# One call instead of two for each head pair's output product in an attention kernel

## The reference, cut to what matters

```python
scores = jnp.einsum('bhqd,bhkd->bhqk', Q, K) / np.sqrt(dh)
x = scores.transpose(0, 2, 1, 3).reshape(b * s, h, s)
x = lax.conv_general_dilated(x, conv_w, window_strides=(1,), padding=[(1, 1)],
                             dimension_numbers=('NCW', 'OIW', 'NCW')) + conv_b[None, :, None]
weights = jax.nn.softmax(x.reshape(b, s, h, s).transpose(0, 2, 1, 3), axis=-1)
out = jnp.einsum('bhqk,bhkd->bqhd', weights, V).reshape(b, s, e) @ Wo.T + bo
```

## Time and profile before

| | us |
|---|---|
| device time, median of 3 runs | 270.06 (269.82 to 270.51) |
| profiled execution, first to last instruction (span) | 268.3 |
| what lies around the span | about 1.8 |
| PE busy in the span | 258.0 (96%) |
| DVE busy | 214.0 (80%) |
| ACT busy | 165.2 (62%) |
| POOL busy | 142.3 (53%) |

### The profile page before, as it was taken

The page is one execution under the profiler, slowest core; times in us unless marked ns, Lnnn a source line. Parts: engine busy times, 40 slices in busy tenths (PEclk is TensorE's granted clock), DMA queues, the critical chain, the costliest instruction groups (busy, mean ns, idle before and its releaser), DMA issues.

```text
span 268.3 us, 5678 instructions
## 1 busy us (share of the span) xinstructions
PE 258.0 (96%) x1835; PEld 191.3 (71%) x1835; DVE 214.0 (80%) x524; ACT 165.2 (62%) x292; POOL 142.3 (53%) x166
## 2 busy tenths in 40 slices
PE   8996989999999999999999999999999999999994
PEld 7455766777777677777667667777676766779982
DVE  2559997988889798888968999889888975686553
ACT  2743887768676776866683577777767771314321
POOL 1029988678687867768482667687863100000000
PEclk9999999999999999999999999999999999999999
DMA  7992000000000000000000000000000000000002
GB/s 222 370 418 85 2 1 1 4 0 0 0 0 0 0 0 0 2 1 2 0 0 2 0 2 0 2 2 0 0 0 0 2 0 2 0 0 4 0 2 78
DMA packets 2964, 8.11 MB, mean 30 GB/s; under 512 B 258, under 2 KB 1794, under 8 KB 2690
## 3 DMA queue, kind: packets, MB, share of 16 engines
q1 hardware_dynamic: 2514, 7.22, 7.2%
q10 hardware_dynamic: 432, 0.65, 0.7%
HBM read 7.34 MB, written 0.52 MB: 29 GB/s over the span
## 4 chain that ended last, share of the span: by engine, by line
PE 82%; DVE 10%; POOL 4%; issue 2%; ACT 1%; DVEq 0%; POOLq 0%; ACTq 0%
PE tp L902 18%; PE sc L777 12%; PE pvbank L794 10%; PE sc L778 9%; PE sc L779 9%; DVE Pb L515 3%; PE sc L993 3%; PE tp L1003 3%; PE sc L721 2%; PE misc L815 2%; DVE PT L631 1%; PE sc L739 1%; PE sc L953 1%; DVE kc L459 1%; PE sc L954 1%
## 5 line engine op out<-in xcount | busy, mean ns | idle before, releaser
L319 ACT ACTIVATE Pb<-Pb,nbias 128x512 f32<-128x512 f32 x128 | 90.7, 721 | 51.5 <-DVE Pb L515 51.0
L515 DVE TENSOR_SCALAR_CACHE_REDUCE Pb<-sc,col 128x512 f32<-128x512 f32 x128 | 93.6, 744 | 19.0 <-PE sc L779 18.3
L902 PE MATMUL tp<-cst,Pb 128*128 128x128 f32 x512 | 76.9, 273 | 0.9 <-DVE PT L631 0.8
L902 PEld LDWEIGHTS tp<-cst,Pb 128*128 128x128 f32 x512 | 63.0, 140 | 20.4 <-issue 1.7
L777 PE MATMUL sc<-Kh,Ql 128*128 128x512 f32 x124 | 60.7, 490 | 0.9 <-POOL Kl L216 0.9
L216 POOL TENSOR_TENSOR Kl<-kc,Kh 128x512 fp32r<-128x512 f32 x29 | 37.5, 1294 | 37.9 <-ACT Kh L314 37.7
L778 PE MATMUL sc<-Kl,Qh 128*128 128x512 f32 x124 | 49.2, 397 | 0.0
L779 PE MATMUL sc<-Kh,Qh 128*128 128x512 f32 x124 | 49.0, 396 | 0.0
L631 DVE COPY PT<-tp 128x512 f32<-128x512 f32 x64 | 43.9, 685 | 1.0 <-PE tp L902 1.0
L228 POOL TENSOR_TENSOR td<-ta,tc_ 128x512 f32<-128x512 f32 x31 | 42.0, 1356 | 2.6
L361 ACT ACTIVATE PT<-tp 128x512 f32<-128x512 f32 x64 | 37.4, 585 | 3.2 <-PE tp L902 2.4
(11 more groups left out here) (232 smaller groups left out, 259.7 us busy)
## 6 DMA issues: line engine op xcount, KB each, us to landing
w1s<-in_w SPq DMA_DIRECT2D x1, 2048.0 KB, 9.6
w2s<-in_w SPq DMA_DIRECT2D x1, 2048.0 KB, 14.0
cst<-in_consts SPq DMA_DIRECT2D x1, 648.0 KB, 5.1
xTs<-in_xT SPq DMA_DIRECT2D x2, 256.0 KB, 3.0
we<-in_wexp SPq DMA_DIRECT2D x2, 256.0 KB, 3.4
b2s<-in_b2row SPq DMA_DIRECT2D x1, 512.0 KB, 14.8
out<-PT SPq DMA_DIRECT2D x2, 192.0 KB, 2.1
wq<-in_wqkvo ACTq DMA_DIRECT2D x1, 320.0 KB, 3.7
```

The costliest lines, as they stand in the source:

```text
L319: act.activation(Pb[:, k, :], Pb[:, k, :], ACT.Exp, bias=nbias[:, k:k + 1], scale=-1.0)\
L515: dve.tensor_scalar(Pb[:, k, :], SC[k % 4][:, :], cb, None, ALU.subtract, ALU.min, accum_out=nbias[:, k:k + 1]).then_inc(s["mx"], 1)
L902: mm = pe.transpose(TP[u % 2][:, k * 128:(k + 1) * 128], Pb[:, u % RING, k * 128:(k + 1) * 128], ident)
```

## The change

A pair's product is one call of `outputs` in u = 1 and in u = 9. It goes through all four tiles of keys, 16 matmul calls or eight rounds, and counts the semaphore `pv` at its end. The calls in u = 3 and 11 are gone. The call's waits are those of the former first half. All other code is the same.

```diff
-            def outputs(hd, j, gi, tiles):
+            def outputs(hd, j, gi):
...
-                for k in tiles:
+                for k in range(QT):
...
-                if k == QT - 1:
-                    mm.then_inc(s["pv"], 1)
+                mm.then_inc(s["pv"], 1)
...
-                if u % (2 * QT) in (1, 3) and not (isinstance(g, int) and b + g == 0 and u < QT):
-                    outputs(H * b + G * g + u // QT - 2, (u // QT - 2) % G, gi - (1 if u < QT else 0),
-                            (0, 1) if u % QT == 1 else (2, 3))
+                if u % (2 * QT) == 1 and not (isinstance(g, int) and b + g == 0 and u < QT):
+                    outputs(H * b + G * g + u // QT - 2, (u // QT - 2) % G, gi - (1 if u < QT else 0))
```

## The result

The changed kernel takes **282.02 us** (median of four runs, 281.59 to 282.17). The kernel before takes 270.28 us (median of four, 269.82 to 272.49). The ratio is 1.041, with a 95% interval of 1.036 to 1.045: slower by 4%. The forecast was 283.0 us, the range 275.5 to 285.5.

What follows compares the result with a forecast made beforehand. PE was taken to set the pace, almost without waits. Losses of 5.4 us for the pairs in u = 9 and 7.6 for those in u = 1 gave +12.9 on 270.06, so 283.0 us; range 275.5 to 285.5.

Steps and rivals of the forecast that it cites:

- What bounds the kernel: Whole loop: PE, busy 96% of the span, sets the pace almost without waits; a unit without a call takes 1.14 us.
- The gain of merging: Each pair's call: four more rounds cost 0.86, the removed half call saves 1.20; gain 0.34 a pair if PE never waits.
- `RAW` in u = 1: u = 1 to 4: PE waits for the copy of `RAW`; loss 0.58 to 1.60 us per regular group, 1.60 taken.
- the upper bound: u = 2: `td` starts 0.05 ahead of `kc`, which takes 1.76, making the group's loss 1.60 instead of 0.58.
- rival B: u = 2 and 10: no `kc` is lengthened, only waits for `RAW` and `Kl` remain; +5.9, 276.0 us; chance 0.12.
- `Kl` in u = 9: u = 9 to 0: late `Kl` holds up the scores of u = 0; loss 0.16 to 0.66 us, 0.66 taken.
- The lower bound, 0.16: u = 9 to 0, without further lengthening of `kc`: 0.70 of the 1.20 comes back against 0.86, so +0.16.
- the case with `kc` first: u = 10, kernel before: `kc` took 1.05 with `td` starting 0.59 into it, said not to fit a full lock.
- rival E: Other units: shifted `kc` and POOL meet there too, or lost PE time stops transposes behind `PT`; above 285.5 us; chance 0.09.
- The irregular groups: Second sequence's first group: 0 in u = 1, +0.86 in u = 9; its second: 0.58 and 0.16; last: 0.58 and 0.86.
- rival C: Whole loop: DVE uses the longer call to get ahead, so neither `RAW` nor `Kl` is late; 265.0 us; chance 0.06.
- Rival A: u = 2: `kc` starts ahead of `td` and keeps 0.75, four times 1.02 less; +8.8, 278.9 us; chance 0.25.

Runs made afterwards that it cites:

- The short: `td` cut from 512 to 64 columns: 273.27 us in the changed kernel, 268.41 us in the kernel before.
- moved `td`: Changed kernel plus a POOL memset of a spare buffer ahead of `td`: 283.20 us with 128 columns, 275.72 us with 512 (the memset kernel).

## Why the prediction was right

The total of 12.9 us stood against 11.7 found by the medians, and no stretch in the table below is a gain. The periods from the scores of u = 2 to those of the next group in the two traces give each term of its sum:

| stretch, from scores of u = 2 to scores of u = 2 | before | after | found | predicted |
|---|---|---|---|---|
| up to the first scores of the loop | | | +0.7 | 0 |
| first sequence, first to second group | 23.55 | 25.26 | +1.7 | 1.72 |
| second to third | 23.64 | 25.90 | +2.26 | 2.26 |
| third to fourth | 23.65 | 25.10 | +1.45 | 2.26 |
| fourth to the second sequence's first | 24.41 | 26.63 | +2.2 | 2.26 |
| second sequence, first to second | 29.28 | 30.16 | +0.9 | 0.86 |
| second to third | 24.47 | 24.50 | +0.03 | 0.74 |
| third to fourth | 23.65 | 25.91 | +2.26 | 2.26 |
| behind the last of them | | | 0.0 | 0.58 |

- **What bounds the kernel**: right. Where PE is not made to wait, the units go on at 1.14.
- **The gain of merging**: 0.34 a pair was right for the place in the changed kernel (1.87 after the call instead of 1.00 is the 0.86 of the term). In another place it was 0.22.
- **`RAW` in u = 1**: the price of 1.60 is right in four of four regular groups. It is 0.86 for the longer call and 5.39 - 4.73 = 0.66 for what the wait took beyond the missing half call; the term had 0.74, since the step from DVE's end to PE's start took 0.06 and not 0.14. The way there is as told: `td` 0.06 ahead (forecast 0.05), `kc` 1.77 to 1.78 (forecast 1.76, from the one row like it). The short and the moved `td` show that the upper bound was right for its reason and that the lower (0.58 each) was real too: take the meeting away and 4.7 to 4.9 us stay, where rival B had 5.9. (By the prediction's own terms B is 6.1: the first group's u = 9 falls from 0.86 to 0.16, by 0.7 and not 0.9.)
- **`Kl` in u = 9**: the price of 0.66 is right in three of the four regular groups (0.65 to 0.69). The lower bound, 0.16, was wrong: with a `kc` of 0.74 the pair gains about 0.15. The prediction read the 1.05 of the earlier trace rows as a `kc` that came first and met `td` on its way; it was a `kc` behind `tc_`, and once the call moves it, the 0.31 between 1.05 and 0.74 comes back as well. The upper bound does not hang on this. The sentence that a full lock does not fit "the case with `kc` first" falls with it: in the traces of the kernels before and after every `kc` that takes more than 0.78 ends 0.53 to 0.55 after the end of a POOL instruction, in all but one case (the 1.26 of u = 6 below) one that had started ahead of it. In the third group `kc` at u = 10 took 0.74, and the term was 0.8 too large. The cause lies in u = 6. There `kc` and `tc_` start within 0.01 of each other in this group and the one before it; in the one before, `tc_` was stretched (1.21, `kc` 0.74), in this one `kc` (rows below), though its recorded start is the earlier one by 0.01. That made `Kh`, `Kl` and all of POOL's work for u = 10 0.51 later against the scores (`td` 2.53 after them instead of 2.02), so `td` came 0.25 behind `kc` (98.25, 98.00). I had not gone through u = 6, which lies between the two calls; rival E named such meetings, but only as a loss.

  Timelines of DVE and POOL of the kernel after, u = 6 of that group:

```profile
91.52 1.26 DVE L459 SCALAR_TENSOR_TENSOR kc<-Kp,col,td 128x512 f32<-128x512 f32 x1
...
91.53 0.71 POOL L223 TENSOR_SCALAR tc_<-Kp,cwS 128x512 f32<-128x512 f32 x1
```

- **The irregular groups**: the second sequence's first came out as told, with `kc` at 0.92. Its second group was priced at 0.58 + 0.16 and cost 0.03. Its `RAW` transposes come 4.69 after the scores of u = 2 (164.06, 168.75) where they came 5.52 after before: DVE had other work waiting there and used the longer call for it. This looks like rival C's mechanism, in the one group where DVE was behind; no run tested it by itself. In u = 10 of that group `kc` started ahead of `td` and took 0.88; the small price for it, 0.16, came to 0. So also the end of the last group, priced at 0.58, cost nothing.
- **Not in the sum**: 0.7 us ahead of the loop. PE waits 0.5 there for the weights `we`, which landed a little later. The experiments have between nothing and 1.1 of it, whatever their edit, so it is a scatter of executions and no part of the change.

The three misses of the terms, 0.8 + 0.7 + 0.6 too much, and the 0.7 of the start leave 1.4 less than the 12.9: the 11.5 of the spans. The forecast was good because the large term was taken from rows that had the same case, a wait for `RAW` and a `kc` with `td` 0.06 ahead. That it came within 1.2 us of the median is in part luck: the 0.7 of the start covers a third of the misses. Rival A's margin of 0.05 stayed a real risk: the memset kernel shows that 0.3 us of shift brings 6.3 us back.

By the Trainium skill (SBUF — State Buffer, Who interferes with whom) `kc` would have waited for `td`'s whole time and then taken its own 0.75, 1.98 in all with `td` 0.06 ahead. The trace of the kernel after has 1.77 to 1.78 five times, so the measurement decides for the smaller size; the direction, and that the one that starts first wins, is as the page says (for starts within 0.01 either was seen to win). The Trainium skill's rule (TensorEngine Tiling (Array Packing), Key Properties) that a change of tiling mode drains the engine fits the 0.22 to 0.34 a pair that a call saved is worth; that this time is the drain, no run shows. And still the kernel was slower by 4%.

## What to carry to other kernels

Longer and fewer calls on the engine that sets the pace save their entry and exit, and make gaps in the supply of the engines that feed it. Before a burst is merged, look up what its followers have queued between the burst and the next thing that the engine needs from them, and put the burst where this queue is empty: here two units later turned +11.7 us into -3.8 us. Do the same for the pairs of instructions on VectorE and GpSimd whose starts lie within some tenths of a microsecond: a shift of a call anywhere upstream decides which comes first, and the later one may take more than twice its time.

## What the runs showed of the hardware

- **The start decides, and the loser ends a fixed time after the winner.** With `td` 0.02 to 0.07 ahead `kc` takes 1.76 to 1.82, with 0.26 ahead 1.58; in the rows shown it ends 0.55 after `td` (86.23 against 85.68, 73.66 against 73.11), less than its own 0.75. Behind `tc_` by 0.18 it takes 1.05 and ends 0.54 after it. With `kc` ahead by 0.28 it keeps its 0.74, and `td` takes 1.59 instead of 1.28, ending 1.13 after `kc` (83.32, 82.19).
- **More work made the kernel faster.** 31 memsets of 0.53 us on POOL brought 6.3 us.
- **A small instruction can vanish.** The memset of 0.20 us ahead of `td` moved `td` by 0.01 to 0.04, since a gap stood there.
- **The price of a column-tiled call depends on what stands beside it.** A half call cost 1.20 between transposes and scores. Two in one unit, one directly behind the scores, cost 2.33 together (3.47 - 1.14), the merged call in that unit 2.11 (3.25 - 1.14), and in u = 1 of the changed kernel 2.04 (82.17 - 78.99 - 1.14).
